# The loop over thirteen middle batches, written out

## The reference

```python
x = layernorm(x + mixer(x))     # per token over 128 features
x = layernorm(x + mixture(x))

# mixer: z = x Wz; B, C, dt, X = split(x Win); delta = softplus(dt + dt_bias)
#   h[t] = exp(-delta[t] exp(A_log)) h[t-1] + X[t] outer (delta[t] B[t])      8 heads, state 64 x 64
#   y[t] = h[t] C[t] + D X[t];  out = (y * (silu(z) Wzg)) Wout
# mixture: a = x P_w^T; dw1, dw2, dw3 = top-3 softmax of a U1^T, a U2^T, a U3^T as rows of 12
#   h = gelu(sum_e dw1[e] * x W1[e]^T);  y = sum_e dw2[e] * h W2[e]^T + dw3 b2
```

## Time and profile before

| what | value |
|---|---|
| median of 3 runs | 1657.14 us (1656.87 to 1659.09) |
| the profiled execution's own time | 1658.27 us |
| its span, first to last instruction | 1656.6 us |
| PE busy | 1563.7 us, 94% |
| VectorE, GpSimd, ScalarE busy | 69%, 39%, 36% |
| DMA, mean over the span | 69 GB/s |
| mean granted TensorE clock | 0.977 of full speed, below 1.00 in the span's first slices alone |

### The profile page before, as it was taken

The page is one execution under the profiler, slowest core; times in us unless marked ns, Lnnn a source line. Parts: engine busy times, 40 slices in busy tenths (PEclk is TensorE's granted clock), DMA queues, the critical chain, the costliest instruction groups (busy, mean ns, idle before and its releaser), DMA issues.

```text
span 1656.6 us, 28375 instructions
## 1 busy us (share of the span) xinstructions
PE 1563.7 (94%) x8466; PEld 1242.3 (75%) x8466; DVE 1139.4 (69%) x3116; ACT 593.8 (36%) x1340; POOL 642.5 (39%) x734
## 2 busy tenths in 40 slices
PE   5459999999999999999999999999999999999997
PEld 3347878778787877778787787877778787787876
DVE  3636667686877768777676777767677776767644
ACT  4434242342424234242433424243342424424130
POOL 4526062352606336161533516144350623526040
PEclk9559999999999999999999999999999999999999
DMA  3513031220403113040321404022040412304020
GB/s 109 154 41 113 21 109 40 62 92 27 127 15 103 55 55 99 26 128 13 94 67 46 108 20 127 20 79 81 31 124 20 116 31 65 89 28 128 20 71 7
DMA packets 81311, 114.36 MB, mean 69 GB/s; under 512 B 10160, under 2 KB 36800, under 8 KB 81216
## 3 DMA queue, kind: packets, MB, share of 16 engines
q1 hardware_dynamic: 81216, 113.45, 23.8%
HBM read 108.28 MB, written 5.13 MB: 68 GB/s over the span
## 4 chain that ended last, share of the span: by engine, by line
PE 72%; issue 11%; POOL 9%; DVE 4%; ACT 2%; DMA 1%; POOLq 1%; DVEq 0%; SPq 0%; ACTq 0%
PE exp_bank L224 18%; PE exp_bank L226 17%; PE exp_bank L225 17%; PE mix_bank L723 4%; POOL sp_lo L938 4%; PE mix_bank L749 3%; PE mix_bank L731 3%; PE mix_bank L224 2%; PE mix_bank L226 2%; PE mix_bank L225 2%; POOL Wt L705 1%; ACT L424 1%; POOL sp_lo L521 1%; PE turn_bank L986 1%; PE mix_bank L831 1%
## 5 line engine op out<-in xcount | busy, mean ns | idle before, releaser
L938 POOL TENSOR_TENSOR sp_lo<-fbuf,sp_hi 128x512 fp32r<-128x512 f32 x192 | 247.3, 1290 | 255.9 <-ACT sp_hi L935 239.5
L224 PE MATMUL exp_bank<-sp_hi,w_hi 128*128 128x512 f32 x768 | 311.8, 406 | 15.9 <-DVE acc L1028 14.8
L224 PE MATMUL exp_bank<-w_hi,sp_hi 128*128 128x512 f32 x768 | 309.8, 403 | 2.0 <-POOL sp_lo L979 2.0
L225 PE MATMUL exp_bank<-w_lo,sp_hi 128*128 128x512 f32 x768 | 303.3, 395 | 0.0
L226 PE MATMUL exp_bank<-w_hi,sp_lo 128*128 128x512 f32 x768 | 303.2, 395 | 0.0
L226 PE MATMUL exp_bank<-sp_hi,w_lo 128*128 128x512 f32 x768 | 303.1, 395 | 0.0
L225 PE MATMUL exp_bank<-sp_lo,w_hi 128*128 128x512 f32 x768 | 301.5, 393 | 0.0
L935 ACT CAST sp_hi<-fbuf 128x512 fp32r<-128x512 f32 x192 | 119.0, 620 | 370.6 <-DVE fbuf L920 301.0
L1025 DVE SCALAR_TENSOR_TENSOR acc<-exp_bank,dw,acc 128x128 f32<-128x128 f32 x384 | 131.7, 343 | 124.9 <-PE exp_bank L226 123.8
L224 PEld LDWEIGHTS exp_bank<-sp_hi,w_hi 128*128 128x128 f32 x768 | 144.6, 188 | 67.6 <-POOL sp_lo L938 22.5
L705 POOL TENSOR_TENSOR Wt<-Wt,Gh 128x512 f32<-128x512 f32 x128 | 176.4, 1378 | 17.1 <-DVE Wt L698 17.1
(11 more groups left out here) (182 smaller groups left out, 2245.5 us busy)
## 6 DMA issues: line engine op xcount, KB each, us to landing
row_b<-dw_rows SPq DMA_DIRECT2D x192, 256.0 KB, 3.4
seg_b<-dA_rows SPq DMA_DIRECT2D x128, 256.0 KB, 3.7
ctd<-cum_rows SPq DMA_DIRECT2D x128, 96.0 KB, 3.3
x_in<-in_x SPq DMA_DIRECT2D x16, 256.0 KB, 2.8
result<-acc SPq DMA_DIRECT2D x16, 256.0 KB, 2.3
fbuf<-in_W1T SPq DMA_DIRECT2D x12, 256.0 KB, 3.5
fbuf<-in_W2T SPq DMA_DIRECT2D x12, 256.0 KB, 2.9
b_sb<-in_b SPq DMA_DIRECT2D x48, 0.5 KB
```

Source lines behind the costliest of these rows:

```text
L224: nc.tensor.matmul(ps, s_hi, m_hi, start=start and j == 0, stop=False)
L225: nc.tensor.matmul(ps, s_hi, m_lo, start=False, stop=False)
L938: sig("xw_lo", PO.tensor_tensor(sp_lo[:, at, :], wide[e % 2], sp_hi[:, at, :].bitcast(F32), ALU.subtract))
```

## The change

The register loop over the batches 2 to 14 is replaced by a Python loop that writes the thirteen bodies out one after another. Each batch's number is then known when the program is made: the waits are on constants, the addresses of input and output are fixed, there are no loop registers and no branches, and the program of every engine is that much longer. Within the thirteen bodies `waited` is now carried from one batch to the next.

```diff
             body(eng, Batch(None, 1), True, norm_before=False)
             waited[id(eng)] = {}
-            with eng.Fori(2, NB - 1) as i:
-                body(eng, Batch(i, 0), True)
+            for i in range(2, NB - 1):
+                body(eng, Batch(None, i), True)
             waited[id(eng)] = {}
             body(eng, Batch(None, NB - 1), False)
             mixture_alone(eng, Batch(None, NB - 1))
```

## The result

The written-out kernel takes 1645.77 us (median of 4 runs, 1645.11 to 1647.35), the kernel before 1657.01 in the same session: ratio 0.9931, 95% interval 0.9914 to 0.9949. It is 0.7% faster, by 11.2 us (by the interval 8 to 14); forecast were 13.9 us less and 1643.3. The profiled execution took 1646.17 us with a span of 1644.4, against 1658.27 and 1656.6 before: 12.1 and 12.2 us less.

The account below looks back on a forecast made before the run. PE, busy 94% of the span, was taken as the bound; 12 x (97.74 - 96.585) = 13.9 us from VectorE's branch, registers, fetches and wait records zero, so 1657.14 - 13.9 = 1643.3 us, range 1639 to 1650.

Parts of the forecast that it names:

- The main step: Batch boundary: VectorE's 2.9 us gap goes in twelve transitions, steps fall from 97.74 to 96.585 us, 13.9 us in all.
- (a): Rival at the batch boundary: gap is a memory wait any version has, no change, 1657.1 us; 5%.
- (b): Rival: only each batch's first 15 us recover, 7.7 us, new fetches keep the row broadcast late, 1649.4 us; 5%.
- (d): Rival on PE: instruction blocks come late, 2.9 us each; one per batch gives 1680.9 us; 5%.
- the row broadcast: Before a later expert: SP issues it late, waiting for VectorE's L920; VectorE idles 1.38 us for row_b, that expert reaches PE late.
- (c): Rival at the batch boundary: the addition chain comes 0.3 us sooner in 13 batches, another 3.9 us, 1639.4 us; 7%.
- the 96.5 to 96.7 that I had named: Sign of being right: all fourteen steps on PE from L749 to L749 take this many us.
- the registers: VectorE's 101 register operations ahead of a batch's waits go: taken as zero, at most 0.3 us a batch.

Follow-up runs that it names:

- hint_dve: Kernel before, loop kept, with a prefetch hint on VectorE's back-edge branch alone: 1644.94 us, ratio to before 0.9922.
- two_bodies: Kernel before with two batch bodies in each loop pass and batch 14 written out, five back edges taken instead of twelve: 1652.75 us, ratio 0.9962.
- one_trip: Kernel before with its loop split into thirteen loops of one pass each, no branch taken back: 1644.96 us, ratio 0.9920.
- late_more: Written-out kernel with six unused statistics instructions on VectorE ahead of batches 3 to 14: 1661.83 us, ratio to before 1.0017.
- hint_late: Loop kernel with the hint on VectorE's branch and five unused statistics instructions on VectorE in each of 13 batches: 1660.36 us, ratio to before 1.0013.
- hi_first: Written-out kernel, PE doing expert 0's eight high-part products first, each bank as soon as its sums are read: 1631.78 us, ratio to before 0.9834.
- row_first: Kernel before, loop kept, SP issuing expert 3's row broadcast ahead of the second half of the rates: 1653.42 us, ratio 0.9968.
- late_end: Written-out kernel with five unused statistics instructions on VectorE in 13 batches, their tile behind all others: 1655.35 us, ratio to before 0.9986.
- hint_hi_first: Loop kernel with the hint on VectorE's branch and PE doing expert 0's high-part products first: 1632.45 us, ratio to before 0.9845.

## Why the prediction was right, and where it was off

The main step, that VectorE's 2.9 us belong to the taken branch and that a batch without them takes 96.585 us, held: 96.61, and hint_dve shows it with everything else of the loop in place. Rivals (a), (b) and (d) fell. (a): the gap went with the hint. (b): the row broadcast did come in time. (d): four or five packets of queue 8 came in every batch and no step was longer than 96.75; two_bodies adds that PE's sequencer has 4.1 us of cover at that place, which I had not counted. (c) fell as argued: the chain at the boundary starts L1028 0.3 us sooner, and it ends with L938 all the same.

Three things were off. First, the size: 13.9 us forecast, 13.6 measured on the marks (steps of 96.61 in place of 96.585, and one of 96.75, just outside the 96.5 to 96.7 that I had named), 12.2 on the span and 11.2 on the medians. The term I had not made is the part outside the thirteen batches: 1.6 us lost at 1.2 GHz in the tail, which the one profile of before did not have. Of the other kernels hint_dve and one_trip have a tail of 121.4 us, late_more 121.9 and hint_late 122.7; the rest have 119.3 to 120.2. The idle time ahead of the last pass doesn't decide it alone: twelve of the kernels have the same 2.25 us there, and the clock falls behind it in five (these four and the kernel after) and not in the other seven. It falls both with a loop (hint_dve, hint_late) and without. Both hi_first kernels, where that idle time is 1.21 us, don't have it; two profiles prove nothing. What decides stays open.

Second, the path. I wrote that the row broadcast is late since SP waits for VectorE's L920. SP did wait, but further up its queue: on L565 for the store of the sums, with six loads behind (row_first). The queue that the lateness passes through was not walked through instruction by instruction, and that would have told which half of the loss can be cured by order alone.

Third, the registers. "Zero" is right for a batch in time (hint_dve). For a late one it is not settled: the loop of hint_late loses 0.26 us a batch more than late_end, but at least 0.16 of it comes with VectorE's instructions at the back edge, the branch among them. The sum was not hurt, since writing out and the hint both take the lateness away.

The pages of the Trainium skill that stood against each other can be judged. The Trainium skill, "Runtime: NRT & Kernel Launch", "Instruction fetch mechanics": that a taken branch can force a fetch before execution goes on is what the trace shows. Its room of 512 instructions for most engines fits hint_dve, whose VectorE pass of 339 is never fetched again, and its 2048 for PE fit 1111 that stay and 2214 that don't. What it doesn't tell is why 338 without the hint don't stay. The Trainium skill's 108 ns for a compare-and-branch ("Advanced Engine Details and Errata", "Control Flow Timing") is no engine's here: the branches take 45 ns on ScalarE, GpSimd and SP, 63 on VectorE and 208 on PE, and with the fetch behind it VectorE's costs 2.9 us.

Left open: what makes VectorE fetch at 338 instructions when GpSimd at 343 doesn't. The place of the loop's first instruction in the program can't be enough: in hint_dve it is the same on VectorE as in the kernel before, 374 instructions in, and nothing is fetched. How far the engine had asked ahead past the loop's end could do it; that was not tried.

## What to carry to other kernels

Look for the two kinds of iteration in a loop's trace: the first and the last, whose back edge isn't taken, show what the rest would take without it. When an engine's next instruction comes microseconds behind its branch, try a prefetch hint on that branch before writing the loop out: here one instruction gave all of it, and the program stayed small. Then follow the late engine's semaphores through every in-order queue that waits on them, SP's above all, since that is where a covered delay comes out again; and a row that "names a DMA" as the end of a wait is worth a look at the sequencer's own instructions in the gap.

## What the runs showed of the hardware that was not expected

- With a hint on its back edge VectorE's loop of 339 instructions fetches nothing (0 packets in twelve passes), without it five packets a pass; the next instruction comes 0.2 instead of 2.7 to 3.0 us behind the branch. It is so in hint_late and hint_hi_first too.
- With 2214 instructions a pass PE's sequencer stands 3.4 to 4.8 us at a back edge, with 1111 it stands 0.2. PE's array didn't notice four times out of five.
- A VectorE addition of 128 columns (L1028) that meets a GpSimd operation on 512 columns ends 0.14 to 0.15 us behind it, however early it starts, in every batch of the kernels before and after and of hint_dve: 0.67 us long in the loop, 1.01 written out, 0.29 when no GpSimd operation runs.
